# Half of a layer norm's scaling moved from VectorE to ScalarE, in a kernel of six interleaved streams

## The reference

```python
def _ln(x):
    mu = jnp.mean(x, axis=-1, keepdims=True)
    var = jnp.var(x, axis=-1, keepdims=True)
    return (x - mu) * jax.lax.rsqrt(var + EPS)
# L0
xm = _ln(x) * (1.0 + sc_sa) + sh_sa;  x = x + g_sa * (attend(q, k, v of xm) @ sa_proj_w + sa_proj_b)
xn = _ln(x);                          x = x + (attend(q of xn, k, v of ctx) @ ca_proj_w + ca_proj_b)
xm = _ln(x) * (1.0 + sc_ff) + sh_ff;  x = x + g_ff * (gelu(xm @ fc1_w + fc1_b) @ fc2_w + fc2_b)
# L1: cross-attention, x and ctx both normalised and modulated
# L2: as L0, with _ln(ctx) on the key side
# L3: nx = layer_norm(x); evidence = softmax(nx Wq (ctx Wk)^T) (ctx Wv); three experts, router, gate; x + g * out
```

## Time and profile before

| | |
|---|---|
| median of 3 runs | 1866.98 us (1864.02 to 1872.07) |
| profiled execution | 1866.06 us, its span 1864.3 us |
| PE / PEld busy | 1756.0 / 1502.5 us |
| DVE busy | 1639.4 us |
| ACT busy | 1383.1 us |
| POOL busy | 643.9 us |
| DMA | 42.62 MB, 23 GB/s |

### The profile page before, as it was taken

One profiled execution on the slowest core, in us unless ns is written; L12 is line 12 of the kernel. 1 busy time (PEld: TensorE's weight loads), 2 busy tenths in 40 slices (PEclk: granted clock), 3 DMA queues, 4 the chain that ended last, 5 costly groups with the idle time before them and its releaser, 6 DMA issues.

```text
span 1864.3 us, 88096 instructions
## 1 busy us (share of the span) xinstructions
PE 1756.0 (94%) x38181; PEld 1502.5 (81%) x38181; DVE 1639.4 (88%) x4236; ACT 1383.1 (74%) x3340; POOL 643.9 (35%) x1145
## 2 busy tenths in 40 slices
PE   3788999999999999999999999999999999999898
PEld 3577788888788888888888888888888888877788
DVE  2898889899899999999999999989999989998874
ACT  1465678787778778777877787878777777777697
POOL 1432323333423333333333333333333333432341
PEclk9899999999999999999999999999999999999999
DMA  4200000000000000000000000000000000000000
GB/s 162 71 14 9 17 23 9 17 23 23 23 23 14 16 19 23 23 23 23 9 17 23 23 23 23 23 3 23 23 23 23 23 13 18 20 11 9 8 5 15
DMA packets 57165, 42.62 MB, mean 23 GB/s; under 512 B 13520, under 2 KB 55632, under 8 KB 56528
## 3 DMA queue, kind: packets, MB, share of 16 engines
q1 hardware_dynamic: 56784, 36.99, 6.8%
HBM read 32.51 MB, written 4.46 MB: 20 GB/s over the span
## 4 chain that ended last, share of the span: by engine, by line
PE 74%; DVE 14%; ACT 6%; issue 3%; DMA 0%; POOL 0%; SPq 0%; DVEq 0%; POOLq 0%
PE half L981 9%; PE half L881 8%; PE half L861 7%; PE half L900 7%; PE half L885 7%; PE half L928 5%; PE half L918 5%; DVE top L1070 4%; PE half L802 4%; PE half L990 4%; PE half L848 4%; PE half L911 3%; PE half L833 3%; PE half L837 3%; ACT pT L1246 2%
## 5 line engine op out<-in xcount | busy, mean ns | idle before, releaser
L761 POOL TENSOR_TENSOR shifted<-moments,eps 128x2 f32<-128x2 f32 x256 | 50.6, 198 | 1027.1 <-DVE moments L1037 1027.0
L1211 ACT ACTIVATE pT<-half 128x512 f32<-128x512 f32 x640 | 328.0, 610 | 102.3 <-PE half L885 101.2
L1070 DVE TENSOR_REDUCE top<-half 128x32 f32<-128x2048 f32 x160 | 365.1, 2282 | 29.4 <-PE half L861 27.8
L881 PE MATMUL half<-o_rows,of_keys 32*128 32x128 f32 x5120 | 273.8, 281 | 5.1 <-ACT o_rows L1163 3.0
L885 PE MATMUL half<-q_heads,k_heads 32*128 32x128 f32 x5120 | 261.4, 271 | 3.0 <-issue 2.9
L1246 ACT ACTIVATE pT<-half,mod 128x64 f32<-128x64 f32 x896 | 196.1, 332 | 50.6 <-PE half L981 49.5
L881 PEld LDWEIGHTS half<-o_rows,of_keys 32*128 32x128 f32 x5120 | 205.9, 186 | 26.3 <-issue 11.5
L885 PEld LDWEIGHTS half<-q_heads,k_heads 32*128 32x128 f32 x5120 | 207.8, 187 | 5.4 <-issue 5.4
L1191 ACT ACTIVATE k_heads<-half,key_bias,own_head_sb 128x256 f32<-128x256 f32 x320 | 163.4, 571 | 47.8 <-PE half L837 46.2
L861 PE MATMUL half<-k_heads,q_heads 32*128 32x128 f32 x5120 | 187.9, 281 | 9.5 <-issue 5.0
L1043 DVE TENSOR_SCALAR n_rows<-x_rows,moments,rstd 128x128 f32<-128x128 f32 x512 | 189.0, 416 | 3.9 <-POOL rstd L763 3.0
(11 more groups left out here) (151 smaller groups left out, 3745.0 us busy)
## 6 DMA issues: line engine op xcount, KB each, us to landing
gates<-gate_store SPq DMA_DIRECT2D x128, 128.0 KB, 3.1
x_rows<-x SPq DMA_DIRECT2D x32, 128.0 KB, 2.2
c_rows<-context SPq DMA_DIRECT2D x32, 128.0 KB, 2.5
out<-x_rows SPq DMA_DIRECT2D x32, 128.0 KB, 1.8
w_sb<-weights SPq DMA_DIRECT2D x1, 2368.0 KB, 12.7
pT<-weights SPq DMA_DIRECT2D x1, 1024.0 KB, 4.7
logit_bias<-logit_store SPq DMA_DIRECT2D x64, 1.5 KB, 3.4
row_sb<-rows SPq DMA_DIRECT2D x1, 769.5 KB, 6.4
```

Source lines behind the costliest of these rows:

```text
L881: nc.tensor.matmul(halves[HALF_OF[n]][:, g, tb * D:(tb + 1) * D], of_keys[part, 2 * tb:2 * tb + 2, :], low[s][part, :], start=True, stop=F ...
L1070: nc.vector.tensor_reduce(top[s][:, :].rearrange("p (g c) -> p g c", c=32)[:, :, 0:2 * GROUP], halves[HALF_OF[n]][:, :, :].rearrange("p g ...
L1211: nc.scalar.activation(turn_cols[s][:, g, :], halves[HALF_OF[n]][:, g, :], ACT.Exp, scale=ATT_SCALE).then_inc(scores_read, 1)
```

## The change

At "normal" VectorE scales only the first 128 rows of a group. GpSimd makes a bias, minus the mean times rstd, for the second 128 rows, at the end of "stats", and ScalarE normalises them at "normal" with Identity, scale and bias. TensorE waits for both at "cols". `SEQUENCE` and `HALVES` are both other strings (same length, same number of steps for each stream, again a period of 546).

```diff
 SEQUENCE = (
-    "0241021000230020202221103203132032010100301132010410310242032021113100231014204130010200113000330240"
+    "0231012000111000210431210102313031202302100023043120142011201403103230022104220310203200101320001330"
...
 HALVES = (
-    "0011110011111100001110011100111100011100000000000111111110000011111100000011111000000111100011100011"
+    "0011110011110011111100110011000011100011111111111000001110000011111110000011111100001111100011100011"
...
+        minus = each("minus", [D, 1])
...
+        minus_in = [sem(f"minus_in{s}") for s in range(STREAMS)]
...
                         nc.gpsimd.tensor_tensor(rstd[s][:, :], shifted[s][:, :], minus_halves[:, 0, :], ALU.pow).then_inc(rstd_in[s], 1)
+                        count.next(rstd_in[s])
+                        nc.gpsimd.tensor_scalar(minus[s][:, :], moments[s][:, 1, 0:1], -1.0, rstd[s][:, 1:2], ALU.mult, ALU.mult).then_inc(minus_in[s], 1)
...
                     if kind == "cols":
-                        count.next(rows_normed[s])
+                        count.next(rows_normed[s], 2)
...
                     if kind == "normal":
                         count.next(rstd_in[s])
-                        for t in range(2):
-                            m = nc.vector.tensor_scalar(n_rows[s][:, t, :], x_rows[s][:, t, :], moments[s][:, t, 0:1], rstd[s][:, t:t + 1],
-                                                        ALU.subtract, ALU.mult)
-                        m.then_inc(rows_normed[s], 1)
+                        nc.vector.tensor_scalar(n_rows[s][:, 0, :], x_rows[s][:, 0, :], moments[s][:, 0, 0:1], rstd[s][:, 0:1],
+                                                ALU.subtract, ALU.mult).then_inc(rows_normed[s], 1)
...
+                    if kind == "normal":
+                        count.next(minus_in[s])
+                        nc.scalar.activation(n_rows[s][:, 1, :], x_rows[s][:, 1, :], ACT.Identity, scale=rstd[s][:, 1:2],
+                                             bias=minus[s][:, :]).then_inc(rows_normed[s], 1)
```

More of the change, by code:

```diff
@@ L181 @@
[L181 to L190, removed]
@@ new lines @@
+    "4210321041320103122031040121301300021110021230101012022001400010204122101421320103211012320104301203"
+    "1200231100141110432104102044022102540341030120351345305201542114351532531122432352422431524015423103"
+    "2310054023012153503132453515440102345315401015342415103245214000345232043332053422503541503525401234"
+    "1243201041524544050425023140255411052425123235103214504531041351134505241053401352025532415305301221"
+    "1451352134031542304310533100420531534204130525540215220341501512440215004401214052230143142130430234"
@@ new lines @@
+    "2014152402430132554433450243123401332504302552010032510530452435105432324045133530253152345150512551"
+    "3221411503210324145243014535034241002405310142450323413211124054231420104402210254034103012035134530"
+    "5201542114351532531122432352422431524015423103231005402301215350313245351544010234531540101534241510"
+    "3245214000345232043332053422503541503525401234124320104152454405042502314025541105242512323510321450"
+    "4531041351134505241053401352025532415305301221145135213403154230431053310042053153420413052554021522"
@@ new lines @@
+    "0341501512440215004401214052230143142130430234201415240243013255443345024312340133250430255201003251"
+    "0530452435105432324045133530253152345150512551322141150321032414524301453503424100240531014245032341"
+    "3211124054231420104402210254034103012035134530520154211435153253112243235242243152401542310323100540"
+    "2301215350313245351544010234531540101534241510324521400034523204333205342250354150352540123412432010"
+    "4152454405042502314025541105242512323510321450453104135113450524105340135202553241530530122114513521"
@@ new lines @@
+    "3403154230431053310042053153420413052554021522034150151244021500440121405223014314213043023420141524"
+    "0243013255443345024312340133250430255201003251053045243510543232404513353025315234515051255132214115"
+    "0321032414524301453503424100240531014245032341321112405423142010440221025403410301203513453052015421"
+    "1435153253112243235242243152401542310323100540230121535031324535154401023453154010153424151032452140"
+    "0034523204333205342250354150352540123412432010415245440504250231402554110524251232351032145045310413"
@@ new lines @@
+    "5113450524105340135202553241530530122114513521340315423043105331004205315342041305255402152203415015"
+    "1244021500440121405223014314213043023420141524024301325544334502431234013325043025520100325105304524"
+    "3510543232404513353025315234515051255132214115032103241452430145350342410024053101424503234132111240"
+    "5423142013423422134041210452503310424015351000514001035255312413542312143501254332205123012434153155"
+    "3205314105230424150324003120512105040430112411140121045211015300041250104515215013504130543543104021"
@@ L206 @@
+    "3425501405034145425120453145011153504150125210352035015244530150035154055440152415301450310431550413"
+    "5010131555034510115034501204535044125001245152015203415441105014310541100112510354312045215344141501"
+    "3414113054105314523145015105413051103302143310041141151301055105340141050505124010104013000104531005"
+    "011100101111"
 )
 HALVES = (
[L208 to L209 removed]
```

25 lines of the change are left out of this document (3 added, 22 removed).

## The result

The changed kernel takes 1858.96 us (median of 20 runs, 1850.74 to 1866.6) against 1867.38 us of the kernel before beside it: ratio 0.9946, 95% interval 0.9933 to 0.9958, 0.54% or some 10 us faster. The forecast was 26 us. The median lies inside the stated range (1812 to 1869), but above the forecast case (1822 to 1857), and what has to be explained is why 16 of the 26 us did not come. Its profiled execution took 1856.2 us, span 1854.4.

What follows compares the result with a forecast made beforehand. TensorE was taken to pace the kernel, VectorE close behind causing most of 131 us lateness. Lateness -31, shape changes -4, VectorE's standing +3, lateness behind ScalarE +7 gave -25 from 1866 us: 1841 us, range 1812 to 1869.

Steps and rivals of the forecast that it cites:

- the forecast case: Whole kernel: 1841 us, 1.4% faster, with 1822 to 1857 us as its span and a chance of 0.58.
- the clean time: TensorE's steps without lateness, 1678 us: changes between whole-array and tiled steps cost 4 us less in the new order.
- VectorE's standing for rstd: VectorE between "stats" and "normal": standing grows from 3.2 to 12.5 us, a third of the growth felt, +3 us.
- ScalarE's wait for the bias: ScalarE at "normal", waiting for GpSimd: under 40 us speaks for the forecast, over 70 for the slower rival.
- rival B: TensorE's lateness passes from VectorE to ScalarE: no change, 1866 us within 9, chance 0.16.
- Lateness -31 (from the shortfalls): TensorE's late steps: new order's longer distances cut shortfalls from 89 to 59 us, counted as 31 us gained.
- the usual cause of the lost 131 us: TensorE's steps, 1809 us as run against 1678 clean: VectorE, close behind TensorE, named as what usually makes them late.
- five kinds of steps: TensorE work between dependent steps against one constant need per kind; shortfalls 89 to 59 us, "normal" to "cols" 25.0 to 4.5.
- lateness behind ScalarE: Values, some maxima products, expert and MLP inputs, keys: some 50 us, to grow by a seventh with ScalarE's load, +7.
- A: VectorE is the true bound, half of the 94.5 us taken off it is felt: 1815 us, chance 0.14.
- C: ScalarE's wait at "normal" holds the banks: 52 places, 72 us standing, half reaching TensorE, +36; 1885 us, chance 0.12.
- D: Transposes at "cols" need both halves, so they are not relieved; no chance of its own, counted in the no-change rival.

Runs made afterwards that it cites:

- e1: Changed kernel with the two order strings of before, so the move to ScalarE alone: 1986.7 us, ratio 1.062 to the kernel before.
- e3: Kernel before (old order) with the normalisation of the second 128 rows left out altogether: 1865.9 us, ratio 0.9979.
- e9: Kernel before (old order) with the normalisation of both halves left out: 1862.0 us, ratio 0.9959.
- x1: Kernel before (old order) with maxima over half of the keys and neither half normalised: 1852.9 us, ratio 0.9913.
- e10: Kernel before (old order) with VectorE's row maxima taken over half of the keys only: 1851.6 us, ratio 0.9935.
- e2: Kernel before with the new order strings alone, both halves staying on VectorE: 1889.4 us, ratio 1.010.
- e4: Kernel before with the new order strings and the second half's normalisation left out: 1861.7 us, ratio 0.9956.
- x4: Changed kernel with Tanh for Gelu and Silu, so ScalarE's table loads fall away: 1849.8 us, ratio 0.9909 to the kernel before.
- x3: Kernel before (old order) with Tanh for Gelu and Silu, so ScalarE's table loads fall away: 1863.7 us, ratio 0.9973.
- s1: Changed kernel (new order and move) in the first 771 steps, kernel before in all others: 1860.9 us, ratio 0.9961.
- e7: Kernel before with GpSimd's bias and ScalarE's wait for it, without ScalarE's instruction; VectorE normalises both halves: 1938.8 us, ratio 1.039.
- e5: Move in the old order, ScalarE's half using constant scale and bias, so without the bias wait: 1942.7 us, ratio 1.039 to the kernel before.

## Why the prediction was right or wrong

**Right in their sizes.** VectorE lighter by 94.5 us (85) and at 86% (87.2), ScalarE's share at 85% (85.3); L1182 0.49 us (0.493 median); table loads 220; the clean time 4 us less (0 to 4); VectorE's standing for rstd 12.5 us (11.8); GpSimd's work free, 0.10 us of waiting and 0.26 for it, 0.36 instead of 0.3. ScalarE's wait for the bias, given as under 40 us, is 41.4, but 17.9 of them are one wait before the first L1182 (in e1 17.1 of 73.5). That 1859 us lies inside the range is owed to the rival B, which the range took in; the forecast case missed it by 2 us.

**The step that failed** is the term "Lateness -31 (from the shortfalls)": measured -4 to -8. Two things were wrong with it.

First its base, the sentence that VectorE is "the usual cause of the lost 131 us". That TensorE waits for a VectorE result is true by name; but e3, e9 and x1 take 77, 159 and 317 us of busy time off VectorE and win 4, 8 and 16. For the maxima e10 shows what does count: their own duration in a short distance (lateness 21 to 6 us). e9, without the normalisation, takes the transposed rows from 24 to 15. For the rest this is argued, not shown. The waits' view names the last releaser and not the reason why it came late.

Second its measure: the distance between five kinds of steps, with one constant need for each, as a count of lateness. Two thirds of the -31 were the distance from "normal" to "cols", 25.0 to 4.5 us, in the steady part 10.2 to 0. The distances did grow so, but the transposed rows are as late as before, 22 to 24 us against 24, and TensorE's waits for a normalised half are 8.8 us against 8.3. In the steady part there was nothing to gain: between 250 and 1500 us the waits of the kernel before show none of TensorE's matmuls for L1043 (its weight loads wait 0.9 us), where the shortfall counted 10.2. And e9, in which nobody normalises anything, still has 15 of the 24 us. Only the transposed maxima did what was said: the shortfall fell from 32 to 24 and the lateness from 21 to between 8 and 10.

Against that gain stands what the list of distances left out. The output projections went from 7.5 to 12 us. The query projections, given as 13.5 to 12.0, went from 8 to between 14 and 18, and 8 of these us are at four places in the steady part, one in each period (333, 666, 995 and 1324 us). At all four the cause is the same, and no kind of step in the list had it: VectorE reaches the "stats" of a stream's next group before its rows have come from HBM, stands there, and behind it in its queue are a maxima instruction and the L1052 that TensorE's query projection needs. At 333 us:

```profile
327.08 0.38 SPq L743 DMA_DIRECT2D x_rows<-x  x1
...
329.31 0.49 DVE L1038 BATCH_NORM_STATS2 stats<-x_rows 128x6 f32<-128x128 f32 x2 [2.82 <-DMA x_rows<-x]
...
329.99 2.26 DVE L1072 TENSOR_REDUCE top<-half 128x32 f32<-128x2048 f32 x1
...
332.62 0.42 DVE L1052 TENSOR_TENSOR nT<-half,mod 128x256 f32<-128x256 f32 x1
...
333.19 1.19 PE L837 MATMUL half<-nT,w_sb 128*128 128x256 f32 x2 [2.34 <-DVE nT L1052]
```

In all, before and after:

```profile
DVE stats L1034 <- DMA x_rows<-x: 3.0, 2, 1.7
...
DVE stats L1038 <- DMA x_rows<-x: 15.1, 8, 2.8
```

Between "store" and the same stream's next "stats" the old order has at least 5.3 us of TensorE work in the steady part, the new one 3.3 at these four places, where the store and the load behind it take 3.35 and 2.10 us in the chain (656.54 and 659.91). Here DMA and SyncE come into the chain, of which they have 3% now and had 0% before. VectorE's waits for these rows are 12 to 18 us in e2, e4 and x4 too, which have the new order. No run moved this one distance by itself, so that its 8 us would be won back is likely and not shown.

Also a part of the lateness was none: within steps, between matmuls that wait for no semaphore, the old order's trace stops 16 times (over 0.5 us from one matmul's start to the next), 14.7 us in all, the changed one 22 times, 21.2 us. A case of the changed kernel, in the middle of 32 maxima products:

```profile
213.41 0.48 PE L865 MATMUL half<-k_heads,q_heads 32*128 32x128 f32 x3
215.33 0.40 PE L865 MATMUL half<-k_heads,q_heads 32*128 32x128 f32 x5 [1.43 <-issue]
```

So of the lateness that distances can mend some 10 us went (by the 127), and 6.5 came back as such stops. The four traces with the whole new order have 18 to 23 of them (18.4 to 23.3 us), the ten with the old order throughout 9 to 17 (9.9 to 18.6), and none of these ten has one in a "v" step, where the new order has 4 to 6 each. What they are is told at the end.

One smaller term was wrong in its working: lateness behind ScalarE was to grow "by a seventh, as its load does from 78.5 to 85%", +7 us. That load grows by a twelfth, which gives +4; the sum would have been 28 us and not 25. x3 and x4, with a fifth less on ScalarE, win 5 and 7 us, so ScalarE's part of the lateness is small either way.

**The rivals.** B ("the lateness only changes hands") describes the mechanism, at a chance of 0.16; its time, 1866 within 9, holds the 1858.96, with clean time and the start (s1, 7 us) as what it had not foreseen. A ("VectorE is the true bound") falls: by its working half of what VectorE lost was to be felt, 47 us, and e3 gave 4. With it falls, for this kernel, the rule of the Trainium skill ("Perfetto Trace Analysis", section "Identifying the Most-Contended Engine") as I applied it, by weight loads alone (the page names the share of peak arithmetic beside them, which I did not work out): TensorE's weight loads at 81% under VectorE's 88% did not mean that VectorE was the engine to relieve; x1's TensorE matmuls stayed at 26920 in the steady 1250 us with VectorE at 74%. What told the bound here was the step times: 1678 of 1809 us are clean.

C ("ScalarE's wait holds the banks behind it") is true where its condition is met, and was priced far too low. I gave 52 places and 72 us of standing a cost of 36 us less the gain, 1885 in all. With the old order ScalarE stands 73.5 us at 35 places, and the time is 1987. With the wait alone (e7) it stands 80 us, 17 of them before its first step, and that costs 70. So ScalarE's standing cost TensorE about its full length and not half of it: what stands behind is work of other streams, and the lower clock after the longer gaps adds to it. I had also left out the second way, that the transposes now depend on how late ScalarE's queue gets there (e5, 74 us). The new order avoids both: its standing is 41.4 us (23.5 without the first wait), and its ratio is that of e4, which has neither wait nor work. This is in keeping with its 7 instead of 31 short distances between "normal" and "cols": that reading of the strings priced no gain, but it says why the move does no harm.

D ("It does not relieve the transposes"), counted in B, came true: the transposed rows are late by 22 to 24 us as before.

**The sum with the measured terms:** clean time 0 to -4; the start, where VectorE's chain share was, -7 (s1, part of the clean time in it); lateness elsewhere 0, where what the maxima gain and what query and output projections lose about cancel. That gives -7 to -11, and the kernels differ by 10.

## What to carry to other kernels

Before pricing relief of an engine by what waits for it, take each step of the bound engine from start to start and see how much is clean: here 93%, and 317 us less on the second engine moved the end by 16. Price the lateness that is left by single distances between steps, each with the queue in front of its producer, and expect it to change hands. Put every input on that list, the loads from HBM too: in an in-order queue the engine that stands for one holds everything behind it. Before a distance is given a price, look whether the trace has the wait that it stands for. A new wait in an in-order queue that serves several streams costs about its standing at the bound engine, unless the order is made for it: the same move cost 116 us with the old order and nothing that can be told with the new, so a move and its order can't be judged apart.

## What the runs showed of the hardware

**TensorE stops for its own instructions.** The page counts the packets of the queue that brings instructions:

```profile
q8 instruction: 306, 5.01, 1.1%
```

That is one packet of 16 KB for every 250 of TensorE's 76362 matmuls and weight loads. The 17 traces have 258 stops of over 0.5 us inside a step (pairs of matmuls that are that long by the lower clock are left out), and every one of them ends 2.15 to 2.93 us (median 2.41) after the start of such a packet, though these stretches are only an eighth of the time. The stop shown above ends at 215.33, and its packet starts at 213.04. They stand in the steps with the most instructions in the shortest time (maxima products, scores, values, "v"). So TensorE runs out of instructions where such steps follow each other closely, and the step order decides how often. That it is the next block of instructions that is waited for is read from the times and not from a record that names it.

**The lower clock comes back in the middle of a busy kernel.** After a gap of 3.6 us TensorE ran 5.6 us at 0.50; in the changed kernel it was busy 2.17 of the 3.60 us in front of such a stretch, which began near 217 us (0.56 over the stretch shown, some of it still at full clock; pairs of L985 take 1.06 us instead of 0.59):

```profile
213.00:216.60 3.60, 2.17 (x69) 1.77 (x58) 2.37 (x9) 2.68 (x8) 1.32 (x3) 1.00 0.02 6
216.60:219.90 3.30, 3.30 (x10) 2.58 (x11) 3.24 (x5) 0.18 (x1) 0.00 (x0) 0.56 0.02 5
...
218.63 1.06 PE L985 MATMUL half<-pT,w_sb 128*128 128x256 f32 x2
...
221.13 0.59 PE L985 MATMUL half<-nT,w_sb 128*128 128x256 f32 x2
```

In front of it was the stop inside a step shown above; the changed kernel's second such stretch begins at 333.0 us, in the 2.34 us wait for L1052. The Trainium skill ("TensorE: Matmul & The Clock Gate", section "HAM oscillation — how this bites in real kernels") tells of TensorE falling back to the lower clock when it waits in the middle of a kernel. The traces agree, with no kernel of this case at under 90% TensorE, and in the changed kernel after shorter waits than e1's 3.6 us. The runs of one kernel differ in it: of the changed kernel's 20, the slowest (1866.6 us) has the lowest mean granted clock, 0.991, and the four at 0.995 and 0.996 take 1852.8 to 1856.1 us. So it is part of their spread of 16 us.

VectorE and GpSimd did not cost each other more than before: L1046 has a median of 339 ns against 342, with one more GpSimd instruction at each normalisation.
